# A graph and mixture-of-experts layer: 32 slots of gathered rows instead of 16, and block sums in a ring of eight

## The chip, the core and the metric

The kernel is one program on one core of a Trainium2 chip. A core has TensorE (PE in the profile), VectorE (DVE), ScalarE (ACT), GpSimd (POOL) and SyncE (SP), which run their own instruction streams and wait for each other through semaphores. The metric is the device time of one execution in microseconds (us), as the median of several.

## The reference

There are 6250 nodes with 256 features and 200000 edges (`src`, `dst`). The edges are stored sorted by `dst`; the graph part reads `row = src` and `col = dst`.

```
xn = layernorm(x)
neigh = xn[col]; w = sigmoid(relu(neigh @ W1 + b1) @ W2 + b2)
gnn = segment_sum(neigh * w, row) / segment_sum(w, row)        # 0 where the weight is 0
x = x + gnn + mix(xn)                                          # mix: linear attention, 8 heads
x = x + experts(layernorm(x))                                  # router, top 2 of 6 experts of 3 layers
```

The gate `w` depends on the node alone. So the kernel makes a table of 6250 rows (padded to 6272) of 257 numbers, `w * xn` and `w`, and the graph part is then a sum of 200000 table rows by `row`.

## The kernel before, in words

**Ahead of the rounds (0 to 498 us).** The edges are packed into keys and sorted by `row` on VectorE, with turns on TensorE. Beside it the layer norm, the gates and the linear attention are worked out. The table goes to HBM (`gated_rows`, `y_table` in the code). The sorted edges are cut into 1563 chunks of 128. A node block is 128 nodes; there are 49 (`BLOCKS`).

**A step** handles one chunk. GpSimd gathers its 128 rows by an indirect DMA (L611) into a slot of `gath_mem`: 128 partitions of 257 numbers, 131.6 KB. VectorE has made a one-hot matrix for it (`mark`, L1274, four at a time). TensorE multiplies the two (`step`, L978), which gives the sums of each node in one of four PSUM banks (`turned`). VectorE adds that bank to the block's sums in `acc_mem` (`add_sums`, L1294). In the profile one step is two matmul records at L978, since an f32 matmul is made in two passes.

**A round** is 32 steps (`STEPS_PER_BLOCK`), and there are 49. Between the steps stands other work, placed by a table of step numbers (`BESIDE`). It is for earlier blocks: `normalise` (ten pieces from step 6 on) turns the sums of the block before into `x2`; the router follows; and the three layers of the six experts of the block two back are spread over the round. Expert `e` has its first layer (L989) after step 5e, its second (L998) after 5e + 2, its third (L1006) after 5e + 4. ScalarE applies bias and relu after the first two (L762), so TensorE waits for ScalarE ahead of the second and the third. VectorE adds the third (L1408). Round 0 and round 1 have no experts.

**What sets the order.** Each engine's instructions are written out in the order of the step numbers. The waits that matter here:

- Indices. ScalarE copies 16 indices at a time into `step_idx` (`stage`, L755), at its place 2 of a round for steps 16 to 31, and at its place 18 for steps 0 to 15 of the next round. GpSimd waits for them once for 16 gathers.
- Slots. There are 16. Step j of a round and step j - 16 share one, so a gather waits until TensorE has done the step 16 back. The waits are made for four slots at a time (`RUNS`), at L606.
- Rows. Each step on TensorE waits for its own rows (`rows_in`), its one-hot matrix, and the add four steps back.

`acc_mem` holds 52 rows of 257 numbers per partition: 49 blocks' sums, one spare and two shared rows for chunks that straddle two blocks. A flag, computed once, chooses a second way of summing (`CUT_ROUNDS`) if the edges are laid out so that a block isn't finished in time. It isn't taken for these inputs.

Of the kernel before, what the change touches and what calls it, by code (L numbers as in the profile page):

```python
# [15 lines left out]
ALU = mybir.AluOpType  # L16
# [6 lines left out]
P = 128  # L23
# [60 lines left out]
SHARED_AT = BLOCKS + 1  # L84

# [84 lines left out]
def gps_layer(nc, a, out, y_table, kept_keys):  # L170
    with ExitStack() as ctx:
# [23 lines left out]
        N_FIELDS = 6  # L195
# [23 lines left out]
        gathered = gath_mem[:, 0:GROUP * ROW].rearrange("p (s n) -> p s n", s=GROUP)  # L219
# [142 lines left out]
        rows_in = [sem(f"rows_in{i}") for i in range(GROUP)]  # L362
# [12 lines left out]
        N_NORM, N_ROUTE = 8, 10  # L375
# [96 lines left out]
        def _(pool):  # L472
# [125 lines left out]
            nc.gpsimd.memset(acc_mem[:, :], 0.0).then_inc(S["acc_zeroed"], 1)  # L598


            def gather_round(i, staged_before, steps=STEPS_PER_BLOCK):
# [17 lines left out]
            with nc.gpsimd.If(pool.value_load(cut_flag[:, :], min_val=0, max_val=1)):  # L619
# [10 lines left out]
                with nc.gpsimd.Fori(0, CUT_ROUNDS) as i:  # L630
                    gather_round(i + BLOCKS, 1)

        @block.scalar
        def _(act):
# [173 lines left out]
            act.wait_ge(S["chunk_step"], 16)  # L808
# [31 lines left out]
        def _(pe):  # L840
# [123 lines left out]
            def step(i, j, marked_before, steps):  # L964
# [4 lines left out]
                slot, group = j % GROUP, j // GROUP  # L969
                for start, end in RUNS:  # L970
                    if slot == start:
                        pe.wait_ge(S["onehot_ready"], STEPS_PER_BLOCK * i + group * GROUP + end + marked_before)
# [3 lines left out]
                missing = sum(k % GROUP == slot for k in range(LAST_STEPS, STEPS_PER_BLOCK)) if marked_before else 0  # L976
                pe.wait_ge(rows_in[slot], 16 * (GROUPS_PER_BLOCK * i + group + 1 - missing))
                nc.tensor.matmul(ps_sum[j % SUM_BANKS], onehot[:, j, :], gathered[:, slot, :], start=True,  # L978
                                 stop=True).then_inc(S["sum_ps"], 1)
# [532 lines left out]
```

## Time and profile before

| | us |
|---|---|
| median of 3 runs | 3126.36 (3113.29 to 3133.15) |
| profiled execution, span from first to last instruction | 3230.1 |
| ahead of the rounds | about 498 |
| rounds (first gather at 498.8, last at 3161.8) | about 2663 |

The page names the span of the profiled execution; the execution's own time outside the span is not given apart, so the span stands for it. It is 3.3% above the median. Busy times overlap between engines. A row of the timeline has the start, the duration, the engine and line, what is written and read, and in brackets how long the engine had been idle and what ended it. "remote" means that the releaser lies in another queue that the view can't name, and "issue" that nothing in the profile explains the idle time. Ends of matmuls are modelled.

### The profile page before, as it was taken

The numbers are of one execution on the slowest core, as the hardware profiler recorded it, in microseconds if no ns is written. First come the engines' busy times: TensorE is split into PE (matmuls) and PEld (weight loads), VectorE is DVE, ScalarE is ACT, GpSimd is POOL, SyncE is SP. The second block draws the span as 40 slices with busy tenths as digits, with TensorE's granted clock in tenths as the row PEclk, the third lists the DMA queues.
The fourth block names the chain that finished last, engine by engine and source line by source line (L and its number), as shares of the span: only waits on it lengthen the run. The fifth ranks groups of instructions, "written<-read, shape, count | busy, mean of one in ns | idle before, by whom it ended". The sixth has DMA issues, their size and how long they took to land.

```text
span 3230.1 us, 46076 instructions
## 1 busy us (share of the span) xinstructions
PE 2222.2 (69%) x11252; PEld 1832.2 (57%) x11252; DVE 1655.7 (51%) x4368; ACT 766.6 (24%) x2128; POOL 1807.8 (56%) x1728
## 2 busy tenths in 40 slices
PE   1567547667767777777777777676676777677777
PEld 1456535455656565566556556565555556565556
DVE  7589895444444444444444444444444444444443
ACT  1334251122222222222222212122222212121223
POOL 3866735655555555555555555555555555555551
PEclk9778768799888988888898889888888988888889
DMA  4000023423223222322232222222222322323220
GB/s 106 0 1 1 1 80 98 125 80 83 80 80 82 79 81 79 83 74 81 80 82 78 80 79 80 80 75 75 76 77 76 83 78 78 82 77 83 74 80 23
DMA packets 106005, 233.25 MB, mean 72 GB/s; under 512 B 31414, under 2 KB 55568, under 8 KB 105962
## 3 DMA queue, kind: packets, MB, share of 16 engines
q0 software_dynamic: 75024, 205.77, 23.7%
q1 hardware_dynamic: 30938, 26.98, 2.7%
q8 instruction: 19, 0.31, 0.0%
q14 instruction: 24, 0.20, 0.0%
HBM read 218.93 MB, written 13.70 MB: 72 GB/s over the span
## 4 chain that ended last, share of the span: by engine, by line
PE 47%; issue 18%; another core or an unknown queue 17%; DVE 6%; ACT 6%; POOL 4%; DMA 1%; DVEq 0%; POOLq 0%; ACTq 0%; SPq 0%
PE turned L978 18%; PE front L1006 10%; PE front L998 9%; PE front L989 8%; ACT feat_mem L762 4%; DVE sort_mem L1165 3%; POOL acc_mem L541 2%; POOL acc_mem L527 1%; PE front L1022 1%; ACT L785 1%; DMA gath_mem<-in_dst 1%; DVE sort_mem L1173 1%; PE front L1038 0%; DVE sort_mem L1179 0%
## 5 line engine op out<-in xcount | busy, mean ns | idle before, releaser
L611 POOL DMA_INDIRECT gath_mem<-gated_rows,step_idx x1563 | 1513.1, 968 | 1180.7 <-PE turned L978 602.7
L1294 DVE TENSOR_TENSOR acc_mem<-acc_mem,turned 128x257 f32 x1563 | 659.1, 422 | 1376.8 <-remote 611.2
L978 PE MATMUL turned<-gath_mem,sort_mem 128*128 128x257 f32 x3126 | 975.5, 429 | 39.4 <-issue 24.4
L762 ACT ACTIVATE feat_mem<-front,b 128x128 f32<-128x128 f32 x1176 | 368.3, 364 | 1950.6 <-remote 986.0
L1006 PE MATMUL front<-feat_mem 128*128 128x256 f32 x1176 | 382.9, 456 | 458.8 <-issue 235.6
L978 PEld LDWEIGHTS turned<-gath_mem,sort_mem 128*128 128x128 f32 x3126 | 616.3, 217 | 133.0 <-issue 45.3
L1006 PEld LDWEIGHTS front<-feat_mem 128*128 128x128 f32 x1176 | 238.8, 221 | 576.4 <-issue 544.6
L998 PE MATMUL front<-feat_mem 128*128 128x128 f32 x2352 | 362.4, 301 | 202.1 <-ACT feat_mem L762 103.7
L998 PEld LDWEIGHTS front<-feat_mem 128*128 128x128 f32 x2352 | 315.1, 205 | 277.9 <-ACT feat_mem L762 140.1
L989 PEld LDWEIGHTS front<-feat_mem 128*128 128x128 f32 x2352 | 366.8, 223 | 28.4 <-ACT feat_mem L762 1.8
L989 PE MATMUL front<-feat_mem 128*128 128x128 f32 x2352 | 360.5, 304 | 1.4 <-ACT feat_mem L762 1.4
L1165 DVE TENSOR_TENSOR sort_mem<-sort_mem 128x320 f32<-128x320 f32 (+2 forms) x568 | 317.9, 640 | 3.0
L1274 DVE TENSOR_TENSOR sort_mem<-lane,tab_mem 128x512 f32<-128x512 f32 (+1 forms) x393 | 271.5, 691 | 17.7 <-DVE feat_mem L1320 11.6
L1408 DVE SCALAR_TENSOR_TENSOR feat_mem<-front,feat_mem 128x256 f32<-128x256 f32 x294 | 140.5, 478 | 18.6 <-PE front L1006 18.6
L541 POOL TENSOR_TENSOR acc_mem<-acc_mem,gath_mem 128x16 f32<-128x16 f32 (+1 forms) x25 | 98.6, 3946 | 75.6 <-ACT acc_mem L676 75.6
L930 PE MATMUL turned<-ident,sort_mem 128*128 128x128 f32 x286 | 63.0, 391 | 93.5 <-DVE sort_mem L1165 91.0
L930 PEld LDWEIGHTS turned<-ident,sort_mem 128*128 128x128 f32 x286 | 50.8, 205 | 102.7 <-DVE sort_mem L1165 99.9
L862 PE MATMUL front<-acc_mem 128*128 128x129 f32 x196 | 33.5, 322 | 70.3 <-POOL acc_mem L549 70.3
L545 POOL TENSOR_TENSOR acc_mem<-acc_mem,gath_mem 128x16 f32<-128x16 f32 (+1 forms) x25 | 74.2, 2968 | 2.0
L862 PEld LDWEIGHTS front<-acc_mem 128*128 128x128 f32 x196 | 28.3, 221 | 71.4 <-POOL acc_mem L549 71.4
L794 ACT ACT_TABLE_LOAD x49 | 62.9, 1283 | 0.9
L785 ACT ACT_TABLE_LOAD x49 | 62.9, 1283 | 0.9
(188 smaller groups left out, 1539.4 us busy)
## 6 DMA issues: line engine op xcount, KB each, us to landing
gath_mem<-gated_rows,step_idx POOLq DMA_INDIRECT x1563
gated_rows<-acc_mem SPq DMA_DIRECT2D x49, 128.5 KB, 2.5
out_rows<-feat_mem SPq DMA_DIRECT2D x48, 128.0 KB
feat_mem<-in_L_ffn_expert_w SPq DMA_DIRECT2D x18, 256.0 KB
base<-in_x SPq DMA_DIRECT2D x1, 3456.0 KB
base<-in_x SPq DMA_DIRECT2D x1, 2688.0 KB, 26.2
kept_keys<-sort_mem SPq DMA_DIRECT2D x1, 832.0 KB, 3.4
gath_mem<-in_src SPq DMA_DIRECT2D x1, 781.2 KB
```

The lines of the kernel that those rows point to most:

```text
L541: nc.gpsimd.tensor_tensor(std[:, 0:heads], var[:, 0:heads], half_power[:, 0:heads], ALU.pow).then_inc(S["pool_step"], 1)
L611: nc.gpsimd.indirect_dma_start(out=gathered[:, slot, :], out_offset=None, in_=y_table, in_offset=bass.IndirectOffsetOnAxis(ap=step_idx[:, ...
L762: nc.scalar.activation(sb_t[:, slot % 2, h, :], ps[:, h, :], ACT.Relu, bias=bias[:, slot, h:h + 1]).then_inc(ready, 1)
L930: last = nc.tensor.transpose(turned[:, at:at + P], held[:, at:at + P], ident[:, :])
L978: nc.tensor.matmul(ps_sum[j % SUM_BANKS], onehot[:, j, :], gathered[:, slot, :], start=True, stop=True).then_inc(S["sum_ps"], 1)
L989: last = nc.tensor.matmul(ps_h1[:, o, :], w1[:, e, h, o * P:(o + 1) * P], this_T[:, h, :], start=(h == 0), stop=(h == 1))
L998: last = nc.tensor.matmul(ps_h2[:, o, :], w2[:, e, h, o * P:(o + 1) * P], h1_T[:, e % 2, h, :], start=(h == 0), stop=(h == 1))
L1006: last = nc.tensor.matmul(ps_y, h2_T[:, e % 2, h, :], w3[:, e, h, :], start=(h == 0), stop=(h == 1))
L1165: nc.vector.tensor_tensor(outs[t], lower, upper, ops[t]).then_inc(sorted_half[half], 1)
L1274: nc.vector.tensor_tensor(onehot[:, at:at + count, :], lane[:, :].unsqueeze(1).broadcast_to([P, count, P]), step_rel[:, bass.ds(step, coun ...
L1294: nc.vector.tensor_tensor(sums, sums, ps_sum[j % SUM_BANKS], ALU.add).then_inc(S["sum_added"], 1)
L1408: nc.vector.scalar_tensor_tensor(y_acc, ps_y, gates[:, e:e + 1], y_acc, ALU.mult, ALU.add).then_inc(S["ey_added"], 1)
```

## The change

The gathered rows have 32 slots. Slot j belongs to step j of every round, so a gather waits for the same step of the round before. The 16 new slots lie in `acc_mem`. That has room because the blocks' sums are no longer kept one per block: block b's sums are in row `b & 7` of a ring of eight, followed by the two shared rows, and then the slots. A ring row must be zero when its next block begins, so `normalise` has a new piece 7 that clears it, once a round, after step 13. The places of the sums are computed with the ring's number (one more small operation and one more field in the set-up). Only the used 10 rows of `acc_mem` are zeroed ahead of the rounds. The second way of summing keeps 16 slots and one row per block.

```diff
+RING = 8
+RING_SHARED_AT = RING
+SLOTS = STEPS_PER_BLOCK
+CUT_SLOTS = GROUP
...
-        gathered = gath_mem[:, 0:GROUP * ROW].rearrange("p (s n) -> p s n", s=GROUP)
+        in_gath = CUT_SLOTS
+        in_acc = acc_mem[:, (RING + SHARED) * ROW:(RING + SHARED + SLOTS - in_gath) * ROW]
+        gathered = [gath_mem[:, s * ROW:(s + 1) * ROW] for s in range(in_gath)]
+        gathered += [in_acc[:, s * ROW:(s + 1) * ROW] for s in range(SLOTS - in_gath)]
...
-        rows_in = [sem(f"rows_in{i}") for i in range(GROUP)]
+        rows_in = [sem(f"rows_in{i}") for i in range(SLOTS)]
...
-            nc.gpsimd.memset(acc_mem[:, :], 0.0).then_inc(S["acc_zeroed"], 1)
+            nc.gpsimd.memset(acc_mem[:, 0:(RING + SHARED) * ROW], 0.0).then_inc(S["acc_zeroed"], 1)
...
-                        pool.wait_ge(S["sum_ps"], STEPS_PER_BLOCK * i + g * GROUP + end + STEPS_PER_BLOCK - GROUP)
+                        pool.wait_ge(S["sum_ps"], STEPS_PER_BLOCK * i + g * GROUP + end + STEPS_PER_BLOCK - slots)
                         pool.nop().then_inc(S["slot_free"], 1)
-                        for slot in range(start, end):
-                            j = g * GROUP + slot
+                        for j in range(g * GROUP + start, g * GROUP + end):
                             if j < steps:
                                 nc.gpsimd.indirect_dma_start(
-                                    out=gathered[:, slot, :], out_offset=None, in_=y_table,
-                                    in_offset=bass.IndirectOffsetOnAxis(ap=step_idx[:, j:j + 1], axis=0)).then_inc(rows_in[slot], 16)
+                                    out=gathered[j % slots], out_offset=None, in_=y_table,
+                                    in_offset=bass.IndirectOffsetOnAxis(ap=step_idx[:, j:j + 1], axis=0)).then_inc(rows_in[j % slots], 16)
...
-                pe.wait_ge(rows_in[slot], 16 * (GROUPS_PER_BLOCK * i + group + 1 - missing))
+                if again is None:
+                    pe.wait_ge(rows_in[j], 16 * (i + 1))
...
-                own = acc_mem[:, bass.ds(ROW * b, ROW)]
+                own_at = ROW * (b & (RING - 1)) if ring else ROW * b
+                own = acc_mem[:, bass.ds(own_at, ROW)]
...
+                if piece == 7:
+
+                    dve.wait_ge(S["sum_added"], SUM_BANKS + steps)
+                    dve.nop().then_inc(S["ffn_pass"], 1)
+                    nc.vector.tensor_copy(own, is_later[:, 0:1].broadcast_to([P, ROW])).then_inc(S["ffn_step"], 1)
+                    dve.wait_ge(S["ffn_step"], links)
+                    dve.nop().then_inc(S["ffn_pass"], 1)
```

GpSimd, the gathers in the loop over the rounds, before: steps 0 to 3, 4 to 7 and so on, one row with the wait and one for the other three.

```order
L606 ISA [waits idx_staged]
L611 DMA gath_mem<-gated_rows,step_idx 128x257 [waits sum_ps]
L611 DMA gath_mem<-gated_rows,step_idx 128x257 x3
L606 REGISTER_ALU
L611 DMA gath_mem<-gated_rows,step_idx 128x257 [waits sum_ps]
L611 DMA gath_mem<-gated_rows,step_idx 128x257 x3
```

The same place now, and the first four of steps 16 to 31 (line numbers are those of the changed kernel).

```order
L616 ISA [waits idx_staged]
L620 DMA gath_mem<-gated_rows,step_idx 128x257 [waits sum_ps]
L620 DMA gath_mem<-gated_rows,step_idx 128x257 x3
L616 REGISTER_ALU
...
L616 REGISTER_ALU [waits idx_staged]
L620 DMA acc_mem<-gated_rows,step_idx 128x257 [waits sum_ps]
L620 DMA acc_mem<-gated_rows,step_idx 128x257 x3
```

The instructions and the semaphores waited for are the same; the number of steps that each wait asks for is 16 lower, and steps 16 to 31 write to `acc_mem`.

VectorE, steps 13 and 14 of a round, before: an add, then the add of the next step.

```order
L1274 TENSOR_TENSOR sort_mem<-lane,tab_mem 128x512
L1290 ISA
L1293 REGISTER_ALU [waits sum_added]
L1294 ISA [waits sum_ps]
L1294 TENSOR_TENSOR acc_mem<-acc_mem,turned 128x257
L1290 ISA
L1293 REGISTER_ALU [waits sum_added]
L1294 ISA [waits sum_ps]
L1294 TENSOR_TENSOR acc_mem<-acc_mem,turned 128x257
L1341 RECIPROCAL feat_mem<-feat_mem 128x1 [waits x2_std]
```

And now:

```order
L1286 TENSOR_TENSOR sort_mem<-lane,tab_mem 128x512
L1302 ISA
L1305 REGISTER_ALU [waits sum_added]
L1306 ISA [waits sum_ps]
L1306 TENSOR_TENSOR acc_mem<-acc_mem,turned 128x257
L1354 REGISTER_ALU
L1356 COPY acc_mem<-is_later 128x257 [waits sum_added]
L1357 REGISTER_ALU
L1305 REGISTER_ALU [waits ffn_step,sum_added]
L1306 ISA [waits sum_ps]
L1306 TENSOR_TENSOR acc_mem<-acc_mem,turned 128x257
L1361 RECIPROCAL feat_mem<-feat_mem 128x1 [waits x2_std]
```

A copy that clears the ring row stands between the adds of steps 13 and 14, and the second add waits for it too.

## Rows read from the trace of the kernel before

**Rows 1.** The page, part 1: each engine's busy time, share and instructions.
```profile
PE 2222.2 (69%) x11252; PEld 1832.2 (57%) x11252; DVE 1655.7 (51%) x4368; ACT 766.6 (24%) x2128; POOL 1807.8 (56%) x1728
```

**Rows 2.** The page, part 5: costliest groups (busy, mean ns | idle before, releaser).
```profile
L611 POOL DMA_INDIRECT gath_mem<-gated_rows,step_idx x1563 | 1513.1, 968 | 1180.7 <-PE turned L978 602.7
L1294 DVE TENSOR_TENSOR acc_mem<-acc_mem,turned 128x257 f32 x1563 | 659.1, 422 | 1376.8 <-remote 611.2
L978 PE MATMUL turned<-gath_mem,sort_mem 128*128 128x257 f32 x3126 | 975.5, 429 | 39.4 <-issue 24.4
L762 ACT ACTIVATE feat_mem<-front,b 128x128 f32<-128x128 f32 x1176 | 368.3, 364 | 1950.6 <-remote 986.0
```

**Rows 3.** Waits of the whole span: who waited for whom, us in total, times, longest.
```profile
POOL gath_mem L611 <- PE turned L978: 602.7, 205, 8.8
POOL gath_mem L611 <- issue: 439.6, 1306, 29.6
POOL gath_mem L611 <- ACT step_idx L755: 94.9, 32, 3.5
```

**Rows 4.** Timelines of GpSimd, TensorE, ScalarE and VectorE, 1488 to 1501 us.
```profile
1488.45 0.95 POOL L611 DMA_INDIRECT gath_mem<-gated_rows,step_idx  x1 [1.79 <-PE turned L978]
...
1493.54 1.10 PE L1006 MATMUL front<-feat_mem 128*128 128x256 f32 x4 [1.39 <-ACT feat_mem L762]
1494.48 0.60 PE L978 MATMUL turned<-gath_mem,sort_mem 128*128 128x257 f32 x2
1494.91 1.05 PE L989 MATMUL front<-feat_mem 128*128 128x128 f32 x8
...
1500.10 0.63 ACT L762 ACTIVATE feat_mem<-front,b 128x128 f32<-128x128 f32 x2 [6.71 <-remote]
1500.12 0.42 DVE L1294 TENSOR_TENSOR acc_mem<-acc_mem,turned 128x257 f32 x1 [2.22 <-remote]
```

**Rows 5.** Timelines of GpSimd and VectorE, a run of sixteen gathers in round 1.
```profile
584.79 0.95 POOL L611 DMA_INDIRECT gath_mem<-gated_rows,step_idx  x1 [2.49 <-PE turned L978]
...
604.06 0.95 POOL L611 DMA_INDIRECT gath_mem<-gated_rows,step_idx  x1 [0.31 <-issue]
...
607.09 0.42 DVE L1294 TENSOR_TENSOR acc_mem<-acc_mem,turned 128x257 f32 x1 [3.76 <-remote]
```

**Rows 6.** Windows of L978: length, PE busy (x), weight loads, clock, DMA share, GB/s.
```profile
1214.00:1219.80 5.80, 1.63 (x6) 1.07 (x6) 0.98 0.29 83
...
1469.50:1475.30 5.80, 2.67 (x10) 1.75 (x10) 1.00 0.31 81
...
1219.80:1225.60 5.80, 1.92 (x4) 1.22 (x4) 0.73 0.42 113
...
1357.00:1362.80 5.80, 0.00 (x0) 0.00 (x0) 0.72 0.35 96
...
1475.30:1481.10 5.80, 1.93 (x8) 1.44 (x8) 1.00 0.35 101
...
590.60:596.30 5.70, 2.58 (x9) 1.27 (x8) 1.00 0.39 108
596.30:607.80 11.50, 3.88 (x7) 1.74 (x8) 0.59 0.34 93
...
1500.10:1506.70 6.60, 2.55 (x6) 1.85 (x6) 0.53 0.27 70
...
1506.70:1511.70 5.00, 2.68 (x11) 1.67 (x10) 1.00 0.23 65
```

**Rows 7.** Timeline of ScalarE: stagings of indices, the first of round 2 and the last.
```profile
614.36 0.22 ACT L755 ACTIVATE step_idx<-tab_mem 128x16 uint32 x1
...
3168.82 0.21 ACT L755 ACTIVATE step_idx<-tab_mem 128x16 uint32 x1
```

**Rows 8.** Lines L1314 and L598: times in ns are least, median and most.
```profile
L1314 DVE COPY acc_mem<-is_later x49: 294/295/511, 577.6 to 3183.3; 128x257 f32 x46, 128x257 f32<-128x257 f32 x3
...
L598 POOL MEMSET acc_mem<- x1: 11237/11237/11237, 458.0 to 458.0; 128x13364 f32 x1
```

More of the change, by code:

```diff
@@ L630, in _ @@
                 with nc.gpsimd.Fori(0, CUT_ROUNDS) as i:
[L631 removed]
+                    gather_round(i + BLOCKS, 1, slots=CUT_SLOTS)
         @block.scalar
@@ L961, in _, with step @@
             nc.tensor.matmul(ps_row_sums, ones[:, :], row_sums, start=True, stop=True).then_inc(S["marks_ps"], 1)
-            def step(i, j, marked_before, steps):
+            def step(i, j, marked_before, steps, again):
                 if j >= steps:
@@ L968, in step @@
                     return
-                slot, group = j % GROUP, j // GROUP
                 for start, end in RUNS:
-                    if slot == start:
-                        pe.wait_ge(S["onehot_ready"], STEPS_PER_BLOCK * i + group * GROUP + end + marked_before)
+                    if j % GROUP == start:
+                        pe.wait_ge(S["onehot_ready"], STEPS_PER_BLOCK * i + j // GROUP * GROUP + end + marked_before)
                 pe.wait_ge(S["sum_added"], STEPS_PER_BLOCK * i + j + 1)
-                missing = sum(k % GROUP == slot for k in range(LAST_STEPS, STEPS_PER_BLOCK)) if marked_before else 0
-                pe.wait_ge(rows_in[slot], 16 * (GROUPS_PER_BLOCK * i + group + 1 - missing))
-                nc.tensor.matmul(ps_sum[j % SUM_BANKS], onehot[:, j, :], gathered[:, slot, :], start=True,
-                                 stop=True).then_inc(S["sum_ps"], 1)
+                if again is None:
+                    pe.wait_ge(rows_in[j], 16 * (i + 1))
+                else:
+                    uses = STEPS_PER_BLOCK // CUT_SLOTS
+                    pe.wait_ge(rows_in[j % CUT_SLOTS], 16 * (BLOCKS + uses * again + j // CUT_SLOTS + 1))
+                rows = gathered[j if again is None else j % CUT_SLOTS]
+                nc.tensor.matmul(ps_sum[j % SUM_BANKS], onehot[:, j, :], rows, start=True, stop=True).then_inc(S["sum_ps"], 1)
             def first_layer(n, e):
@@ L1007, in third_layer, with pe_round @@
                 last.then_inc(S["ey_ps"], 1)
-            def pe_round(i, n, steps, experts, lead, mixing=False, marked_before=0, here=STEPS_PER_BLOCK):
+            def pe_round(i, n, steps, experts, lead, mixing=False, marked_before=0, here=STEPS_PER_BLOCK, again=None):
                 places = BESIDE if steps else ALONE
@@ L1294, in add_sums, with normalise, shared_sums @@
                 nc.vector.tensor_tensor(sums, sums, ps_sum[j % SUM_BANKS], ALU.add).then_inc(S["sum_added"], 1)
-            def shared_sums(b):
-                return acc_mem[:, bass.ds(SHARED_AT * ROW + ROW * (b & (SHARED - 1)), ROW)]
-            def normalise(n, b, steps, piece):
+            def normalise(n, b, steps, piece, ring):
                 links = FFN_LINKS * n + piece + 1
-                own = acc_mem[:, bass.ds(ROW * b, ROW)]
+                own_at = ROW * (b & (RING - 1)) if ring else ROW * b
+                own = acc_mem[:, bass.ds(own_at, ROW)]
+                def shared_sums(b):
+                    return acc_mem[:, bass.ds((RING_SHARED_AT if ring else SHARED_AT) * ROW + ROW * (b & (SHARED - 1)), ROW)]
                 if piece == 0:
@@ L1382, in route, with dve_round @@
                     nc.vector.tensor_tensor(gates[:, :], gate_1[:, :], gate_2[:, :], ALU.add).then_inc(S["gates_ready"], 1)
-            def dve_round(i, t, n, block_at, steps, experts, lead, all_steps=STEPS, here=STEPS_PER_BLOCK):
+            def dve_round(i, t, n, block_at, steps, experts, lead, all_steps=STEPS, here=STEPS_PER_BLOCK, ring=True):
                 places = BESIDE if steps else ALONE
@@ L1409, in dve_round @@
                     if lead and places["norm"] <= j < places["norm"] + NORM_PIECES:
-                        normalise(n + 1, block_at, STEPS_PER_BLOCK * i + j + 1 if steps else all_steps, j - places["norm"])
+                        normalise(n + 1, block_at, STEPS_PER_BLOCK * i + j + 1 if steps else all_steps, j - places["norm"], ring)
                     if lead:
```

46 lines of the change are left out of this document (24 added, 22 removed).

## The prediction

> **What bounds the kernel now.** I read the page first, then the waits, then the timeline of one round, then the step matmuls (L978) by windows.
>
> No engine is full: in the page's first part TensorE's matmuls have 69% and GpSimd 56% [rows 1]. The groups show what the 49 rounds are made of: 1563 gathers issued at L611, 1563 steps (two passes each, 3126 matmuls at L978), 1563 adds at L1294 [rows 2]. Two things stand out. TensorE idled only 39.4 us in all ahead of its step matmuls, so it hardly ever waits for rows. And VectorE's adds and ScalarE's relus (L762) idle for 1376.8 and 1950.6 us, much of it put down to "remote", a releaser that the view can't name.
>
> The waits say how GpSimd issues. Of the 1563 gathers, 1306 begin 0.3 us after the one before (439.6 us over 1306), so 257 come after a real wait: for a step's slot (205), for the indices that ScalarE stages at L755 (32), or one not named [rows 3]. A run of gathers without a wait is thus 1563 / 257 = 6.1 long on average; the timeline shows mostly eights and fours, since four slots are freed at a time.
>
> The timeline of one round shows what a run does to the others [rows 4]. GpSimd starts a run of eight at 1488.45. TensorE's records go on: L1006 at 1493.54, step 10 of this round at 1494.48, the first layer (L989) at 1494.91, whose eight passes should be over at 1496.0. But the relu that waits for L989 starts at 1500.10 after 6.71 us of "remote", and the add that waits for step 10 at 1500.12, 5.6 us after that step began. Both are let go together, 11.65 us after the run's first gather: 1.46 us for each of eight. The run of sixteen that begins at 584.79 ends its last issue at 605.0; adds in it stand 3.76 us and more behind, and at 607.09 and later they are released in quick order, some 23 us after the first issue, 1.44 us each [rows 5]. So I read it thus: **while gathers follow each other without a pause, TensorE's completions reach the other engines late, and this lasts until the run has landed.** What the hardware does there the trace doesn't say. I take the pattern, not a cause.
>
> What it costs is in the windows of L978 (two matmuls are one step) [rows 6]. Over the 13 runs of eight that start between 1213 and 1477 us, the first 5.8 us have 127 matmuls, 4.9 steps a run; the next 5.8 us have 47, 1.8 steps, 0.31 a us. First and last of each are shown, and the lowest, with none. In the run of sixteen the stretch from 5.8 to 11.5 us has 9 matmuls and the last 11.5 us have 7, 3.5 steps, 0.30 a us, though that round has no expert layers. After a run TensorE begins slowly: 6 matmuls in 6.6 us at a granted clock of 0.53 (the 1.2 GHz level for most of it; it had stood idle before), then 11 in 5.0 us at 1.00.
>
> A round is now (3168.82 - 614.36) / 46.5 = 54.9 us, from one staging of indices to another 46.5 rounds later [rows 7].
>
> **The change, part by part.**
>
> *Slots.* With 32 slots the wait for a slot is met before the indices are there: step j of a round needs step j of the round before. What holds a gather is the staging alone, at ScalarE's places 2 and 18, for 16 gathers at once. The 205 waits for a step go; GpSimd's issue order stays. Each round then has two runs of sixteen instead of about five shorter ones. Gathers were not late, so being earlier gives nothing: at most the 39.4 us of [rows 2] over the whole kernel, and I take 0, since "issue" and the adds end those.
>
> *The run of sixteen.* Its hold lasts 16 x 1.445 = 23.1 us [rows 5]. Steps in it: 4.9 in the first 5.8 us, then 17.3 us at 0.31, 5.4 more, 10.3 together. The 16 steps of a half round leave 5.7 for after the run: three in 6.6 us, 2.7 more at 5.5 in 5.0 us, 2.5 us, so 9.1 us. A half round is 32.2 us, a round 64.4, 9.5 more than 54.9. Over the 46.5 rounds that is +442 us. Bounds of the held rate: above, the 8 steps in the 17.2 us of the sixteen without experts, 0.47 a us: 13.0 steps in the run, 3.0 after it, 6.6 us, a round of 59.4, +209 us. Below, nothing at all after 5.8 us, as in the lowest window: 11.1 steps left, 6.6 + 7.4 us, a round of 74.2, +897 us. I take 0.31, since both the eights' second halves and the end of the sixteen give it. If recovery is at full clock at once, the 9.1 us become 5.2 and the +442 falls to about +80; the one round with three slow steps is the nearest row, so I keep it, and this end is kept for the range.
>
> The first two rounds have runs of sixteen already (that at 584.79 is one), and carry no experts: 0, at most +10 us.
>
> *The copy at piece 7.* VectorE clears the block's ring slot once a round, between steps 13 and 14: 49 copies of 128x257. Its like, L1314, takes 295 ns, 511 at most [rows 8]. 49 x 0.3 = 15 us of VectorE, hidden by its 1376.8 us of idle time before adds; TensorE may run four steps ahead of an add. The wait in it is for adds already made, and the queue behind it (the add of step 14, then the norm) is held by the same 0.3 us. If that cover is gone, 15 us, at most 25.
> The Trainium skill (SBUF — State Buffer, "SBUF: two separate sides") says that a VectorE copy between SBUF tensors locks GpSimd out of writing descriptors while it lasts. By that rule the copy would also hold up one gather a round by its own 0.3 us, 15 us in all at worst, already the bound above.
>
> *Set-up.* The memset of the sums shrinks from 13364 columns, 11.2 us, to 2570 [rows 8], about 2.2 us. It ends at 469.2, and the first gather starts only at 498.8, so the 9 us were hidden: 0. One more small VectorE operation on 13 columns ahead of the places: less than one add of 422 ns [rows 2], once: 0.
>
> **Sum.** 3230.1 + 442 = 3672 us in the profiled execution. That execution is 3.3% above the median of 3126.36, so I carry the growth over at the same ratio, 428: **3555 us**, 14% slower.
>
> **Rivals.**
> *A, no change.* Long runs cost no more than short ones: the hold depends on how many gathers are in the air, and both versions have 32 a round, 32 x 1.445 = 46 of 54.9 us. Then the lost steps are the same and the time is 3126, 3140 with the copy. For it: the mean of the held rate is the same in the eights' second half as late in the sixteen. Against it: each run has 5.8 good microseconds at its start (4.9 steps against 1.8), and five starts become two.
> The Trainium skill bears on this one (same page and section): it says engine ports and DMA ports of SBUF are separate, a DMA can't be slowed by compute or the other way round, and TensorE never waits on anyone. By that rule the runs' length is nothing to TensorE and the time stays at 3126 us. The trace doesn't agree: completions stand 5 us late in a run [rows 4]. 7%.
>
> *B, faster.* Each run costs one hold of fixed length, however long it is. In an eight, 5.8 us at 1.8 steps instead of 4.9 lose 3.7 us. With 257 / 49 = 5.2 runs a round, and 2 after, 3.2 x 3.7 = 11.8 us go. The gathers' own 46.4 us is the floor, so a round would be 46.4, 8.5 less: -395 us, about 2745. It decides if a sixteen runs at more than 0.64 steps a us after its first 5.8 us (all 16 steps then fit in 23.1 us), which the best eight did (8 matmuls in 5.8 us from 1475.3, 0.69) and the other twelve did not. Against it, 0.30 measured at the end of a sixteen. 8%.
>
> *C, slower by little.* The held rate is as in A's reading of the light round (0.47) and recovery is quick: a round of 56 to 59, 3180 to 3330. I count it in the forecast.
>
> That the change would not do what it says (runs stay short) I give 1%: nothing else on GpSimd's queue waits.
>
> **Chances.** Forecast 84%, with its own ends from +80 to +897 (3200 to 4000); A 7%, B 8%. About 1% (31 us) is what a measurement of this kernel can tell from no change. Faster 0.08, same 0.08, slower 0.84. The range leaves out A, B and the far ends: 3230 to 3900.
>
> **What would show it.** L611 should wait some 98 times instead of 257, almost all for L755, for about 12 us each (half a round less 16 x 1.25 us, some 1150 us in all), and none for a step. Stagings at L755 stand 32 us apart on average. In a run, L1294 and L762 wait for "remote" up to 23 us after its first issue, and their "remote" sums grow by several hundred us. L978 has some 20 matmuls in the first 23 us of a half round, and the mean granted clock falls. TensorE's wait ahead of L978 stays small. I'm wrong if L978 runs above 0.5 steps a us late in a sixteen, if the releases don't fall at 1.44 us times the run's length, or if the rounds are 55 us or less.

## The result, and the profile after

The changed kernel takes 3776.61 us (median of 4 runs, 3763.16 to 3777.62); the kernel before, in 4 runs on the same chip, 3119.82 us (3102.93 to 3133.15). The ratio is 1.209, with a 95% interval of 1.202 to 1.215. The forecast was 3555 us, in a range of 3230 to 3900. All ratios are of fast runs alone; of e2's ten runs below, five were over 1.5% above the fastest and are left out of its ratio, though not out of its median.

The profiled execution has a span of 3761.3 us, against 3230.1. Its page, part 1, against [rows 1]: each engine does the same work, in a smaller share of a longer span. The mean granted clock fell from 0.855 to 0.777.

```profile
PE 2259.7 (60%) x11252; PEld 1883.6 (50%) x11252; DVE 1652.5 (44%) x4418; ACT 763.0 (20%) x2128; POOL 1787.9 (48%) x1728
```

The waits of the whole span (who waited for whom, us in total, times, longest us), against [rows 2, 3]. L771 is the relu that was L762, L1306 the add that was L1294, L620 the gather that was L611, L990 the step that was L978, L764 the staging that was L755.

```profile
ACT feat_mem L771 <- remote: 1412.7, 169, 15.0
DVE acc_mem L1306 <- remote: 939.6, 192, 11.0
...
PE front L1009 <- ACT feat_mem L771: 837.9, 91, 13.6
...
POOL gath_mem L620 <- PE turned L990: 632.4, 48, 16.7
POOL acc_mem L620 <- PE turned L990: 628.3, 101, 15.1
```

The relus' idle time put down to "remote" grew from 986.0 to 1412.7 us, the adds' from 611.2 to 939.6. Outside TensorE the instructions are as long as before (an add 421 ns against 422, a relu 364 in both), and TensorE's own, at the lower clock, add up to 2259.7 us instead of 2222.2. The rest of the 531 us is work that starts later. TensorE's second layer (L1009) now waits 837.9 us for relus that had themselves been kept waiting.

The timeline of GpSimd, ScalarE, VectorE and TensorE over one run of sixteen gathers, as [rows 4, 5] showed an eight and a sixteen (start, duration, instruction, and in brackets the idle time before and what ended it):

```profile
1085.23 1.47 POOL L620 DMA_INDIRECT acc_mem<-gated_rows,step_idx  x1 [13.49 <-PE turned L990]
...
1090.14 1.16 PE L1009 MATMUL front<-feat_mem 128*128 128x128 f32 x8
...
1096.93 0.63 ACT L771 ACTIVATE feat_mem<-front,b 128x128 f32<-128x128 f32 x2 [6.85 <-remote]
...
1097.70 2.05 PE L1017 MATMUL front<-feat_mem 128*128 128x256 f32 x4 [5.53 <-issue]
...
1100.55 0.42 DVE L1306 TENSOR_TENSOR acc_mem<-acc_mem,turned 128x257 f32 x1 [7.37 <-remote]
...
1104.68 0.95 POOL L620 DMA_INDIRECT acc_mem<-gated_rows,step_idx  x1 [0.30 <-issue]
...
1104.75 0.42 DVE L1306 TENSOR_TENSOR acc_mem<-acc_mem,turned 128x257 f32 x1 [2.46 <-remote]
...
1108.33 0.63 ACT L771 ACTIVATE feat_mem<-front,b 128x128 f32<-128x128 f32 x2 [10.77 <-remote]
1108.34 0.42 DVE L1306 TENSOR_TENSOR acc_mem<-acc_mem,turned 128x257 f32 x1 [3.09 <-remote]
...
1109.01 2.07 PE L1009 MATMUL front<-feat_mem 128*128 128x128 f32 x8 [5.99 <-ACT feat_mem L771]
```

GpSimd issues from 1085.23 to 1105.6. The relu that needs L1009, whose last pass should end at 1091.3, starts at 1096.93, 11.70 us after the first gather. Two adds are let go in between, at 1100.55 and 1104.75. The next relu, and an add within 0.01 us of it, start at 1108.33, 23.10 us after the first gather: 1.44 us for each of sixteen, as the forecast had it. Only then can TensorE begin its next second layer, at 1109.01.

The trace also records each update of a semaphore, which the views don't print, and there the delay can be seen itself. From 1091 us to the end of the run TensorE ends eight matmuls that signal another engine: L1009 at 1091.30, two steps by 1092.17, L1017 at 1099.75, a step at 1100.61, L1000 at 1102.15 and two steps by 1103.02. Their updates come in the same order, at 1096.91, 1100.43 and 1104.63, and then five together from 1108.17 to 1108.39: 5.4 to 12.5 us after the matmuls' modelled ends. The last gather's landing is recorded at 1107.40, before those five. The signal the other way isn't late here: the two relus that start at 1096.93 are over at 1097.56, and L1017 starts at 1097.70. So it is TensorE's completions that stay back, in their order.

Over the runs in which an add or a relu waits for "remote", the last such wait ends at about 1.44 us times the run's length: as a median 5.75 us after the first gather for 41 fours of the kernel before, 11.57 for 128 eights, and 22.85 for 88 sixteens of the changed kernel, 85 of which lie within 0.25 us of 23.0.

Windows of the step matmuls (L990) in that run and the next (window, its length, PE busy (x), weight loads, granted clock, DMA share, GB/s), to be laid beside [rows 6]. For each run: the first 5.8 us, the rest up to 23.1 us, and the time to the next run's first gather.

```profile
1085.23:1091.03 5.80, 2.67 (x10) 1.76 (x11) 1.00 0.25 68
1091.03:1108.33 17.30, 3.13 (x10) 2.04 (x10) 0.71 0.37 99
1108.33:1118.23 9.90, 4.46 (x14) 2.97 (x15) 0.81 0.00 0
1118.23:1124.03 5.80, 2.76 (x10) 1.66 (x10) 1.00 0.31 83
1124.03:1141.33 17.30, 1.73 (x6) 0.98 (x6) 0.75 0.35 94
1141.33:1150.77 9.44, 4.65 (x14) 2.96 (x14) 0.74 0.04 14
```

Two matmuls are a step. Counted in this way over the 76 runs of sixteen between 1000 and 3600 us, a run has 5.0 steps in its first 5.8 us, 3.9 in the next 17.3, and 7.1 after them, in 10.1 us; from one run's first gather to the next one's are 33.2 us. In the quarters of the 23.1 us (5.8 us each) it has 5.0, 2.5, 1.3 and 0.14 steps: the run dries up.

Stagings of indices, the same two as in [rows 7] (the sixth of 99, and the last); between them are 46.5 rounds again:

```profile
L764 ACT ACTIVATE step_idx<-tab_mem x3: 214/216/216, 615.3 to 681.7; 128x16 uint32 x3
...
3700.02 0.21 ACT L764 ACTIVATE step_idx<-tab_mem 128x16 uint32 x1
```

(3700.02 - 615.3) / 46.5 is 66.3 us a round, against 54.9. The 11.4 us more, 46.5 times, are 530 us; the spans differ by 531.

The two smaller edits, against [rows 8] (least, median and most in ns; L1356 is the new copy at piece 7, L608 the memset):

```profile
L1356 DVE COPY acc_mem<-is_later x49: 293/295/298, 574.3 to 3720.9; 128x257 f32 x46, 128x257 f32<-128x257 f32 x3
...
L608 POOL MEMSET acc_mem<- x1: 2241/2241/2241, 449.8 to 449.8; 128x2570 f32 x1
```

### The profile page after: what moved, and what is told of

It reads as the page before. It is cut to its first block, busy times and chain, and to the rows that moved or that the text cites. A ratio compares the mean times of both kernels' runs of the same rounds, so it can differ in the third digit from the quotient of the medians.

```text
span 3761.3 us, 46362 instructions
## 1 busy us (share of the span) xinstructions
PE 2259.7 (60%) x11252; PEld 1883.6 (50%) x11252; DVE 1652.5 (44%) x4418; ACT 763.0 (20%) x2128; POOL 1787.9 (48%) x1728
## 4 chain that ended last, share of the span: by engine, by line
another core or an unknown queue 39%; PE 35%; issue 11%; ACT 7%; DVE 4%; POOL 3%; DMA 1%; DVEq 0%; POOLq 0%; SPq 0%; ACTq 0%
PE turned L990 13%; PE front L1009 9%; PE front L1017 6%; PE front L1000 5%; ACT feat_mem L771 4%; DVE sort_mem L1176 3%; POOL acc_mem L551 2%; ACT L803 2%; POOL acc_mem L537 1%; PE front L1033 1%; DMA gath_mem<-in_dst 1%; DVE sort_mem L1184 0%; ACT feat_mem L803 0%; PE front L1044 0%
## 5 line engine op out<-in xcount | busy, mean ns | idle before, releaser
L1306 DVE TENSOR_TENSOR acc_mem<-acc_mem,turned 128x257 f32 x1563 | 658.0, 421 | 1922.6 <-remote 939.6
L620 POOL DMA_INDIRECT gath_mem<-gated_rows,step_idx x784 | 747.5, 954 | 887.1 <-PE turned L990 632.4
L620 POOL DMA_INDIRECT acc_mem<-gated_rows,step_idx x779 | 763.3, 980 | 840.5 <-PE turned L990 628.3
L1009 PE MATMUL front<-feat_mem 128*128 128x128 f32 x2352 | 415.9, 331 | 855.5 <-ACT feat_mem L771 837.9
L771 ACT ACTIVATE feat_mem<-front,b 128x128 f32<-128x128 f32 x1176 | 368.2, 364 | 2365.4 <-remote 1412.7
L1009 PEld LDWEIGHTS front<-feat_mem 128*128 128x128 f32 x2352 | 360.9, 232 | 935.4 <-ACT feat_mem L771 892.5
L1017 PE MATMUL front<-feat_mem 128*128 128x256 f32 x1176 | 408.8, 482 | 314.9 <-issue 209.1
L990 PE MATMUL turned<-gath_mem,sort_mem 128*128 128x257 f32 x1568 | 504.0, 435 | 31.1 <-DVE acc_mem L1306 15.3
L990 PE MATMUL turned<-acc_mem,sort_mem 128*128 128x257 f32 x1558 | 488.2, 427 | 46.5 <-issue 40.3
L1017 PEld LDWEIGHTS front<-feat_mem 128*128 128x128 f32 x1176 | 270.5, 243 | 414.7 <-issue 364.3
L990 PEld LDWEIGHTS turned<-gath_mem,sort_mem 128*128 128x128 f32 x1568 | 322.5, 225 | 82.1 <-issue 20.3
L1000 PEld LDWEIGHTS front<-feat_mem 128*128 128x128 f32 x2352 | 347.4, 212 | 25.9 <-ACT feat_mem L771 1.8
L990 PEld LDWEIGHTS turned<-acc_mem,sort_mem 128*128 128x128 f32 x1558 | 303.7, 216 | 100.4 <-issue 57.8
L1000 PE MATMUL front<-feat_mem 128*128 128x128 f32 x2352 | 342.9, 294 | 1.4 <-ACT feat_mem L771 1.4
L1176 DVE TENSOR_TENSOR sort_mem<-sort_mem 128x320 f32<-128x320 f32 (+2 forms) x568 | 308.9, 607 | 3.0
```

The source lines that it names most:

```text
L620: nc.gpsimd.indirect_dma_start(out=gathered[j % slots], out_offset=None, in_=y_table, in_offset=bass.IndirectOffsetOnAxis(ap=step_idx[:, j ...
L771: nc.scalar.activation(sb_t[:, slot % 2, h, :], ps[:, h, :], ACT.Relu, bias=bias[:, slot, h:h + 1]).then_inc(ready, 1)
L990: nc.tensor.matmul(ps_sum[j % SUM_BANKS], onehot[:, j, :], rows, start=True, stop=True).then_inc(S["sum_ps"], 1)
L1000: last = nc.tensor.matmul(ps_h1[:, o, :], w1[:, e, h, o * P:(o + 1) * P], this_T[:, h, :], start=(h == 0), stop=(h == 1))
L1009: last = nc.tensor.matmul(ps_h2[:, o, :], w2[:, e, h, o * P:(o + 1) * P], h1_T[:, e % 2, h, :], start=(h == 0), stop=(h == 1))
L1017: last = nc.tensor.matmul(ps_y, h2_T[:, e % 2, h, :], w3[:, e, h, :], start=(h == 0), stop=(h == 1))
```

## The experiments

The theory: the long unbroken runs of gathers cost the time, since completions stay back until a run lets go. The rivals: the ring, the copy or the rows' new place cost it; or the hold is a matter of bytes, of spacing, or of the number of rows. The groups e, f, g and h ran on four different chips, each with the kernel before beside it, and that turned out to matter more than anything else. The record doesn't name the result's chip; by its times (3120 us for the kernel before, not 3230 or 2550) it is counted as a fifth. A chip that keeps completions back in this way is called a holding one below. Each was used at one time only, so what belongs to the chip and what to its state at that time isn't told apart.

| kernel | median us | before, same chip | ratio, 95% |
|---|---|---|---|
| e1: change, waits of 16 slots | 3221.63 | 3229.77 | 0.996 (0.992 to 1.000) |
| e2: change, issues 1.44 us apart | 3287.19 | 3229.77 | 1.012 (1.008 to 1.017) |
| e3: before, issues 1.44 us apart | 3101.90 | 3229.77 | 0.962 (0.956 to 0.969) |
| e4: change, 512-byte rows | 3852.59 | 3229.77 | 1.194 (1.184 to 1.204) |
| f1: change, issues 1.60 us apart | 3093.39 | 2548.62 | 1.216 (1.211 to 1.220) |
| f3: change, SyncE fills the slots | 2249.02 | 2548.62 | 0.884 (0.881 to 0.886) |
| f4: change, 64 rows a gather | 2492.14 | 2548.62 | 0.976 (0.971 to 0.982) |
| f5: change, plain transfers by GpSimd | 2242.68 | 2548.62 | 0.880 (0.878 to 0.883) |
| g1: the change itself | 2549.71 | 2546.43 | 1.001 (1.000 to 1.003) |
| h1: f1 again | 3097.32 | 2550.19 | 1.215 (1.213 to 1.218) |
| h2: f3 again | 2248.87 | 2550.19 | 0.883 (0.881 to 0.885) |
| h3: f4 again | 2487.77 | 2550.19 | 0.974 (0.970 to 0.978) |

### e1: the change with the waits of sixteen slots

```diff
-                        pool.wait_ge(S["sum_ps"], STEPS_PER_BLOCK * i + g * GROUP + end + STEPS_PER_BLOCK - slots)
+                        pool.wait_ge(S["sum_ps"], STEPS_PER_BLOCK * i + g * GROUP + end + STEPS_PER_BLOCK - GROUP)
```

> The changed kernel with all its parts (ring of eight sums, the copy at piece 7, 32 slots in memory), but GpSimd's waits ahead of a run of gathers are those of sixteen slots: gather j waits for step j-16, four at a time. Theory (the length of the unbroken runs of gathers is what costs): runs are again fours and eights, 200 or more waits for a step, and the time is that of the kernel before, 3120, at most 3150 with the copy. Rival 1 (the ring, the copy or where the rows now lie costs it): still 3700 to 3780, with few or many waits. Rival 2 (half and half): between 3250 and 3600.

Its ratio is 0.996. Its waits (as above) are those of the kernel before:

```profile
ACT feat_mem L771 <- remote: 959.7, 194, 8.1
...
DVE acc_mem L1306 <- remote: 581.9, 183, 7.1
...
POOL gath_mem L620 <- PE turned L990: 336.1, 111, 7.4
POOL acc_mem L620 <- PE turned L990: 263.6, 93, 6.9
```

204 waits for a step, where [rows 3] have 205, and "remote" sums of 959.7 and 581.9 where [rows 2] have 986.0 and 611.2. The ring, the copy, the memset and the new place of the slots are all in this kernel, and together they cost nothing. What costs is that GpSimd no longer waits for a slot. Rivals 1 and 2 fall, on one condition: the change itself was never timed on this chip. That long runs cost time here too is shown by e4, next.

### e4: half the bytes

```diff
-                                    out=gathered[j % slots], out_offset=None, in_=y_table,
+                                    out=gathered[j % slots][:, 0:128], out_offset=None, in_=y_rows,
```

> The changed kernel, but each gather fetches only 128 of the 257 columns (rows of 512 bytes instead of 1028, from a view of the table with rows of that length; the other columns of the slots stay zero, so the sums are not the reference's). As many gathers, runs and descriptors, half the bytes. Theory (backlog of landing): a gather of 512-byte rows lands in 0.5 to 0.9 us, below the 1.25 us of its issue, so nothing is held, and the time falls below 3000. Rival (issuing itself or the number of gathers in a run holds them): still 3700 to 3780.

The backlog I expected isn't there. Half the bytes gave 1.194, nearly what the change with full rows has on its own chip (1.209). GpSimd, ScalarE and VectorE over one run of e4, and two windows behind its last issue (window, length, PE busy (x), weight loads, VectorE, ScalarE, GpSimd, clock, DMA share, GB/s):

```profile
1506.19 0.95 POOL L626 DMA_INDIRECT acc_mem<-gated_rows,step_idx  x1 [12.52 <-PE turned L996]
...
1529.02 0.63 ACT L777 ACTIVATE feat_mem<-front,b 128x128 f32<-128x128 f32 x2 [14.26 <-remote]
```

```profile
1526.20:1527.40 1.20, 0.00 (x0) 0.00 (x0) 0.00 (x0) 0.00 (x0) 0.00 (x0) 0.50 0.20 55
1527.40:1529.20 1.80, 0.00 (x0) 0.00 (x0) 0.04 (x1) 0.18 (x1) 0.00 (x0) 0.50 0.00 0
```

The last packets move before 1527.40, 21.2 us after the first issue; from there the DMA share is 0.00. The release comes at 1529.02, 22.8 us after it, as with full rows. Beside e1, which has short runs on the same chip and 0.996, this shows that the long runs cost the time. In the full run of sixteen shown above it is the same: after 1107.43 the DMA engines are idle, and the release comes 0.9 us later.

```profile
1106.43:1107.43 1.00, 0.00 (x0) 0.00 (x0) 0.00 (x0) 0.00 (x0) 0.00 (x0) 0.50 0.32 103
1107.43:1108.33 0.90, 0.00 (x0) 0.00 (x0) 0.00 (x0) 0.00 (x1) 0.00 (x0) 0.50 0.00 0
```

So the rows follow their issues, 1.25 us apart, and don't pile up. What takes 1.44 us a gather isn't the moving of bytes.

### e2 and e3: issues 1.44 us apart

After each gather of the blocks' rounds (here in the change, and alike in the kernel before, where the gather has `rows_in[slot]`):

```diff
+                                if PAUSE and slots == SLOTS:
+                                    pool.wait_ge(S["paused"], STEPS_PER_BLOCK * i + j + 1)
+                                    pool.nop().then_inc(S["slot_free"], 1)
+                                    nc.gpsimd.memset(tab_mem[32:64, 2 * COLS + 400:2 * COLS + 400 + PAUSE], 0.0).then_inc(S["paused"], 1)
```

> The changed kernel with a small memset on GpSimd (32 partitions x 256 columns) after each gather of the blocks' rounds, which the next gather's issue follows, so that gathers are issued further apart: 1.6 to 1.8 us instead of 1.25. Each run of sixteen keeps its length in gathers. Theory (completions are held because gathers are issued faster, 1.25 us, than they land, 1.44 us, so that a backlog is there to the end of the run): with spacing above 1.44 us no backlog forms, completions come within 2 us, the 'remote' idle ahead of the relus falls from 1412.7 to below 500, and the time falls below 3100, perhaps 2800. Rival (completions are held as long as gathers of any kind are in the air, whatever their spacing): runs last 26 to 29 us, the hold with them, and the time is 3776 or above, up to 4100. Rival 2 (GpSimd's own time for descriptors is what holds them): held for the same GpSimd-busy time, no change, 3776 within 2%.

> The kernel before with the same pause after each gather. Theory (backlog): fours and eights land as they are issued, no hold, the time falls below 3000. If hold goes with gathers in the air whatever the spacing: 32 pauses a round of some 0.4 us are 13 us more of a held time, 3120 rises to 3300 or more. If only GpSimd's descriptor time counts: 3120 within 2%.

The spacing came out shorter than I had put it, 1.44 us. Even so nearly the whole loss is gone: 1.012, where e4 on this chip has 1.194; and in the kernel before the same pause gives 0.962, 128 us less for 32 x 0.19 us more of issuing in a round. Both rivals (hold as long as gathers are in the air; hold by GpSimd's own time) wanted the same or more. The gain is smaller than I wrote, though: I had put e2 below 3100 where the kernel before takes 3120, a ratio under 0.994, and "remote" ahead of its relus is 1143.5 us, not under 500; e3 reached 0.962, just what 3000 against 3120 is. The theory behind it, a backlog of rows, had fallen with e4. VectorE and ScalarE in one run of sixteen of e2, whose gathers are issued from 1548.78 to 1571.4:

```profile
1554.77 0.42 DVE L1315 TENSOR_TENSOR acc_mem<-acc_mem,turned 128x257 f32 x1 [2.30 <-PE turned L999]
...
1559.92 0.62 ACT L780 ACTIVATE feat_mem<-front,b 128x128 f32<-128x128 f32 x2 [3.24 <-remote]
1560.76 0.42 DVE L1315 TENSOR_TENSOR acc_mem<-acc_mem,turned 128x257 f32 x1 [2.06 <-remote]
...
1567.93 0.62 ACT L780 ACTIVATE feat_mem<-front,b 128x128 f32<-128x128 f32 x2 [7.39 <-remote]
```

Releases come within the run now, though some still stand 7 us back. Over 47 such runs the stretch from 5.8 to 23.1 us has 8.2 steps instead of 3.9. At a spacing of just the 1.44 us in question completions get past often, not always. Since the runs are as long in gathers as before (57 of its 101 runs are of sixteen, some are longer), it isn't their length alone that costs, but length at 1.25 us apart.

### f1, f3, f4 and f5: a chip that holds nothing

```diff
f1:-PAUSE = 256
f1:+PAUSE = 440
f3:+                                sp.dma_start(gathered[j], y_table[j * P:(j + 1) * P, :]).then_inc(rows_in[j], 16)
f4:-                                    out=gathered[j % slots], out_offset=None, in_=y_table,
f4:-                                    in_offset=bass.IndirectOffsetOnAxis(ap=step_idx[:, j:j + 1], axis=0)
f4:+                                    out=gathered[j % slots][0:64, :], out_offset=None, in_=y_table,
f4:+                                    in_offset=bass.IndirectOffsetOnAxis(ap=step_idx[0:64, j:j + 1], axis=0)
f5:+                                    nc.gpsimd.dma_start(gathered[j], y_table[j * P:(j + 1) * P, :]).then_inc(rows_in[j], 16)
```

> The changed kernel with a longer pause on GpSimd after each gather (a memset of 440 columns instead of 256), which should put the issues some 1.6 us apart instead of 1.44. In e2 the spacing was 1.44 us, just the 1.44 us at which a run without pauses lets go (16 gathers, 23 us), and TensorE's updates still came up to 3.5 us late. Theory (something serves a gather in 1.44 us, whatever its bytes, and TensorE's updates pass only when it has nothing left): at 1.6 us there is free time after each gather, the updates come within 1.5 us of the matmul throughout, and the time falls below e2's 3287 on the same chip, to 3050 or less. Rival (time lost goes with the time that gathers take in all): runs are 25.6 us instead of 22.8, the round grows, and the time is 3350 or more.

> The changed kernel, but SyncE loads the slots with plain transfers of 128 consecutive rows of the table (1028 bytes each, as many bytes, at the same waits), not GpSimd with gathers by index; GpSimd issues the loads of the experts' weights and the stores of the output in turn. The rows aren't those of the edges, so the sums are not the reference's. Theory (GpSimd's making of descriptors is what holds TensorE's updates): with none made, no hold: updates within 0.1 us of the matmul, mean granted clock above 0.9, and a time of 2400 to 2800. Rival (the transfers into the slots or their completions hold them): bursts of sixteen transfers hold the updates as before, 3500 or more.

> The changed kernel, but each gather fetches 64 rows instead of 128 (the other 64 partitions of a slot stay zero, so the sums are not the reference's): half the descriptors, full rows. e4 halved the bytes and kept the 128 descriptors, and nothing changed. Theory (1.44 us is the time for 128 descriptors): updates of a run of sixteen are released well before 23 us, near 12 to 16 us if the issue gets shorter too, and the time falls below 3300. Rival (the cost is one per gather, not per row): release still at 23 us after the first issue, 3700 to 3800.

> The changed kernel, but GpSimd fills a slot with a plain transfer of 128 consecutive rows instead of a gather by index, same bytes, waits and queue (the sums are not the reference's). Theory (making descriptors in software holds the updates, whether by index or not): if its issue takes as long as a gather's, the hold stays and the time is above 3500; if the issue is shorter than 0.5 us, the hold shrinks with it and the time falls below 3000. Rival (reading the indices is what matters): no hold at all at the same issue time.

These four ran on a chip where the kernel before takes 2549 us, not 3230. In the traces of f1, f3 and f5 none of TensorE's 2903 updates of a semaphore stands more than 0.02 us behind the end of its matmul; in f4 24 have no record near them (20 of those are of one matmul, L1050). No wait of any engine in the four is put down to "remote". So these runs can't say what holds updates, and my expectations of what would let them go weren't tested. They do show what is left without a hold. f1's 1563 gathers at 1.60 us are 2501 us, and about 490 us come ahead of them: 2991 of its 3093. With the gathers gone from GpSimd (f3, f5) the time is 2249 and 2243, and TensorE's matmuls are busy for 87% of the span: the gathers' issue is the bound on such a chip. f4 is 2.4% faster: its issues stand 1.21 us apart instead of 1.25, so an issue costs by the gather and hardly by its rows.

### g1: the change itself on a chip that holds nothing

> The changed kernel itself, once more beside the kernel before, because the chips differ: on the chip of e1 to e4 the kernel before took 3230 us, on that of f1 to f5 only 2549, and no update of TensorE came late in any trace taken there. 2549 us is close to what GpSimd's issues alone need: 1563 gathers 1.25 us apart are 1954 us, and the first gather starts about 500 us in. Theory (the change costs time only through the held updates): where the kernel before takes about 3120 to 3230, the change again costs 19 to 21% and its runs of sixteen let go at 23 us; where the kernel before takes about 2550, there is no hold, the gathers' issue bounds both, and the change is within 1% of it, or a few per cent faster. Rival (the longer runs or the copy cost something of their own): slower by over 2% on such a chip too.

1.001, with an interval of 1.000 to 1.003. Its page, part 5 (busy, mean ns | idle before), and the gathers' line (ns least, median, most):

```profile
L1306 DVE TENSOR_TENSOR acc_mem<-acc_mem,turned 128x257 f32 x1563 | 658.5, 421 | 690.3 <-PE turned L990 531.9
...
L771 ACT ACTIVATE feat_mem<-front,b 128x128 f32<-128x128 f32 x1176 | 367.2, 363 | 1331.2 <-PE front L1000 806.1
L990 PE MATMUL turned<-gath_mem,sort_mem 128*128 128x257 f32 x1568 | 498.0, 407 | 135.1 <-DMA gath_mem<-gated_rows,step_idx 119.7
```

```profile
L620 POOL DMA_INDIRECT gath_mem<-gated_rows,step_idx x784: 942/946/2325, 488.9 to 2474.7; - x196
L620 POOL DMA_INDIRECT acc_mem<-gated_rows,step_idx x779: 942/946/1407, 511.2 to 2489.1; - x195
```

This is the same program, with the instructions of the other engines as long as before: the add 421 ns, the gather 946 ns (949 in the result's trace). TensorE's are shorter, 407 ns a step's matmul instead of 435, with a mean granted clock of 0.948 instead of 0.777; it idles less. Its gathers make one unbroken run of 1563, the longest possible, and nothing is held: "remote" is gone from the relus' and adds' rows. What an add waits for is a matmul that isn't done, and TensorE waits for rows (119.7 us of 135.1 ahead of these steps), which on a holding chip came to 2.6 us at most (e1). From staging to staging a round is 41.0 us, of which 32 issues at 1.25 us are 40.0. So a back-to-back run of gathers doesn't hold completions by itself; it does so on some chips and not on others.

The Trainium skill (SBUF — State Buffer, "SBUF: two separate sides") says that engine ports and DMA ports can't contend and TensorE never waits on anyone. The traces of g1, f and h agree. Those of the forecast, the result and e show gathers delaying other engines all the same, up to 15.0 us for "remote"; but what comes late there is a semaphore's update, after its matmul, and the section speaks of ports and not of updates. So they don't refute it, and it doesn't give the cause.

### h1 to h3: the three that mattered, again

> The kernel of f1 once more, since the chip of f1 held nothing: the changed kernel with the pause of 440 columns, issues 1.60 us apart. There it took 3093 us in one unbroken run of gathers, 1563 x 1.60 us and 500 us ahead of them, 21% above a kernel before of 2549. If this chip holds (the kernel before at 3100 to 3250): by the theory (TensorE's updates pass only when the 1.44 us per gather leave free time) the updates come within 1.5 us and the time is 3090 to 3150, below e2's 1.012 times the kernel before, about 0.96. By the rival (hold goes with the time in which gathers run) it is above 3300. If this chip doesn't hold (the kernel before at 2550), 3093 again, and nothing is told.

> The kernel of f3 once more: SyncE fills the slots with plain transfers of 128 consecutive rows, GpSimd makes no gathers (the sums are not the reference's). Where nothing was held it took 2249 us, 0.884 of the kernel before. If this chip holds: by the theory (GpSimd's gathers hold the updates) 2240 to 2350 again, 0.70 to 0.73 of a kernel before of 3200. By the rival (transfers into the slots, or their completions, hold them, whoever issues) updates come late in each burst and the time is above 2700.

> The kernel of f4 once more: gathers of 64 rows instead of 128 (the sums are not the reference's), issues 1.21 us apart. Where nothing was held it took 2492 us. If this chip holds: by the theory (1.44 us is the time for 128 rows, so 64 take 0.7 to 1.0 us, less than the 1.21 us between issues) the updates pass between gathers and the time is 2490 to 2900. By the rival (the cost is one per gather, whatever its rows) a run of sixteen lets go at 23 us and the time is 3600 or more.

This chip held nothing either (the kernel before: 2550.19), and the times repeat those of f to 0.2%. What on a holding chip takes 1.44 us a gather, rows or the gather as such, GpSimd's descriptors or the transfers' completions, stays open: the runs that would tell met no such chip.

## Why the prediction was right, and where it was off

**What bounds the kernel.** Right for the chips on which the profile and the result were taken: completions reach the other engines late while gathers follow each other. The part "until the run has landed" was wrong. The packets end 0.9 us and more before the release (above, and e4). I had tied the hold to them because both last about as long.

**Slots.** Right. 90 of the 99 runs are of sixteen, and the waits for a step of the same round are gone. The signature I gave was half wrong: GpSimd's waits of some 13 us are put down to L990, not to the staging, because the view names one releaser of two and the staging itself waits for a step. Their sum was to be 1150 us and is 1260.7.

**The run of sixteen.** This is the term that was mis-sized. The hold's 23.1 us came out, though the row named for them gives less: the add at 607.09 in [rows 5] starts 22.30 us after its run's first gather, 1.39 us each, while the eight of [rows 4] gives 1.46. The start came out too: 5.0 steps against 4.9. In the 17.3 us behind it I took 0.31 steps a us from the eights [rows 6], 5.4 steps; measured are 3.9, 0.23 a us. In every second run only three steps pass (6 matmuls in the window from 1124.03). I had taken the eights' second halves for the steady rate of a hold, and there is no steady rate: by quarters of a sixteen it is 0.43 steps a us in the second, 0.22 in the third and 0.02 in the last. TensorE finishes what it already may start and what an occasional release lets through, and then stands, 5.99 us ahead of L1009 in the timeline above. My lower bound (nothing at all after 5.8 us) allowed for it; my value didn't. The two rates may be from two chips, but that isn't the reason: e4's sixteens, on the chip where the kernel before takes 3230 us, have 3.5 steps in their 17.3 us.

**After the run.** 5.7 steps in 9.1 us were forecast, 0.63 a us; 7.1 in 10.1 us came, 0.70 a us. The slow restart is there (clock 0.81 and 0.74 in the two windows). Together a half round is 33.2 us, not 32.2, and a round by the stagings 66.3, not 64.4: 530 us more in the span instead of 442.

**From the profiled execution to the median.** This cost more than the hold's term. I took the 3.3% between the span of 3230.1 and the median of 3126.36 for a cost of profiling and scaled the growth down to 428 us; against the kernel before on its chip it is 657. Profiling adds nothing here: the profiled runs of the change and of e1 are among their timed ones, with spans 1.9 and 1.8 us below their times (3761.3 of 3763.16, 3223.5 of 3225.3). The span of before fits none of the four times on the result's chip (3102.93 to 3133.15), but a chip on which the kernel before takes 3215.12 to 3250.20 us exists (that of e). So the profile of before probably comes from another chip than its times. That is argued, not shown; what the change itself costs on the chip of e wasn't measured, and the nearest is e4's 1.194.

**The copy, the memset, the set-up.** Taken at nothing; e1 has all of them and 0.996. The copy takes 295 ns, as its like did. The gathers that run beside a copy are 0.04 us longer on average than the others in g1 (48 of them) and 0.11 us in e1 (45), not 0.3: 2 and 5 us in all, inside the bound of 15. With the shorter memset the first gather starts at 481.4 us instead of 498.8, and nothing of that is left at the sixth staging (615.3 against 614.36).

**The rivals.** B, a fixed hold for each run, falls: the sixteen's late rate is 0.23 a us, not over 0.64, and fewer runs cost more. A, that length costs nothing, falls on the holding chips by e1 and e4. Its time, no change, is just what comes out on a chip that holds nothing, for a reason that it didn't give (g1). The profile of one chip couldn't show that the result hung on the chip, so that "slower" came true is in part luck: on the chip of g1 the same change gives 1.001.

**A version that beats both?** On the chip of e, the kernel before with a pause of 0.2 us does, by 3.8%. On the chips of f, g and h the gathers' issue is the bound, and a pause costs: that of f1, 0.35 us, 21.6% (h1: 21.5%). The pause of 0.2 us wasn't run there; by the same sum, 1563 gathers 1.44 us apart after some 490 us, my estimate is 2741 us, over 7% more. So no pause that was run is shown to be better on both.

## What to carry to other kernels

A wait for a buffer can be what keeps a kernel fast: before it is removed, look at what the other engines do while the queue behind it runs unbroken, and extend a rate measured in short bursts to long ones only after asking how much of it was work that was ready beforehand. When "remote" idle time stands ahead of engines whose inputs should be there, time the kernel on a second chip before tuning around it; here one program took 2547 us on one chip and 3230 on another. If gathers are issued from one queue in dense runs, spacing them at the rate at which they let go gained 3.8% on a chip that holds; on one that doesn't, where the issue is the bound, a pause is a plain loss.

## What the hardware showed that I had not expected

- The kernel before takes 3120 us on the result's chip, 3230 on that of e, and 2546 to 2550 on those of f, g and h. Outside TensorE the instructions are as long on a holding chip as on the others (the add 421 ns in the result and in g1).
- On the chips that hold, a run of gathers lets go at about 1.44 us times its length after its first issue (medians of 5.75, 11.57 and 22.85 us for four, eight and sixteen), whether its rows have 1028 or 512 bytes (22.96 us for sixteen), while the issues stand 1.25 us apart and the packets end by 21.2 to 22.2 us in the two runs shown.
- What is late is TensorE's update of a semaphore, up to 12.5 us behind its matmul in the run shown, and the updates keep their order. Before the last release single ones get through; then five came within 0.22 us.
- A gather of 128 rows by index keeps GpSimd 0.95 us and 1.25 us apart from the next; one of 64 rows stands 1.21 us apart; a plain transfer of as many bytes keeps GpSimd 0.55 us.
